# Attention exponentials of a decoder layer: the bf16 high part written by ScalarE instead of cast by VectorE

## The reference

```python
x = x + attn(layernorm(x))        # 16 query heads of width 128, one shared key and value head
x = x + experts(layernorm(x))     # 4 experts, picked by token id
x = x + ffn(layernorm(x))         # bit-quantized linear, GELU, bit-quantized linear
# inside attn, q and k normalized to length 4:
sim  = einsum('bhid,bjd->bhij', q, k)
attn = softmax(sim)
out  = einsum('bhij,bjd->bhid', attn, v)
```

## Time and profile before

| | |
|---|---|
| median of 3 runs | 1022.97 us (1019.31 to 1026.55) |
| the profiled execution | 1022.3 us |
| its span, first to last instruction | 1020.6 us |
| TensorE matmul busy | 923.6 us (90%) |
| VectorE busy | 701.5 us (69%) |
| ScalarE busy | 623.2 us (61%) |
| mean granted TensorE clock | 0.972 |

### The profile page before, as it was taken

One profiled execution on the slowest core, in us unless ns is written; L12 is line 12 of the kernel. 1 busy time (PEld: TensorE's weight loads), 2 busy tenths in 40 slices (PEclk: granted clock), 3 DMA queues, 4 the chain that ended last, 5 costly groups with the idle time before them and its releaser, 6 DMA issues.

```text
span 1020.6 us, 18975 instructions
## 1 busy us (share of the span) xinstructions
PE 923.6 (90%) x6524; PEld 519.3 (51%) x6540; DVE 701.5 (69%) x1544; ACT 623.2 (61%) x1595; POOL 272.4 (27%) x402
## 2 busy tenths in 40 slices
PE   4698899899999999999999999999847879999973
PEld 2254566556556655656656556565313334444431
DVE  6778877776886876888676767784353457777852
ACT  4666767767667756676667666664112368888550
POOL 3222212112332424324232222310240012223321
PEclk9899999999999999999999999999978989999997
DMA  8534553657768554456444434469729956444341
GB/s 237 135 73 94 115 105 82 165 146 194 178 156 197 118 141 114 109 128 121 111 97 120 104 94 120 99 140 215 173 93 175 205 120 146 98 105 106 82 103 51
DMA packets 305598, 131.85 MB, mean 129 GB/s; under 512 B 275232, under 2 KB 279840, under 8 KB 305504
## 3 DMA queue, kind: packets, MB, share of 16 engines
q1 hardware_dynamic: 301584, 117.77, 52.0%
q0 software_dynamic: 3920, 12.86, 3.8%
HBM read 42.76 MB, written 20.99 MB: 62 GB/s over the span
## 4 chain that ended last, share of the span: by engine, by line
PE 56%; DVE 18%; ACT 10%; issue 6%; DMA 5%; SPq 3%; POOL 2%; ACTq 0%; DVEq 0%; POOLq 0%
DVE P L1110 6%; PE S L673 5%; PE OUTB L685 5%; PE QB L238 4%; PE QB L239 4%; PE QB L240 4%; PE S L238 4%; PE S L239 4%; PE S L240 4%; DVE P L1108 3%; PE O L572 3%; PE O L570 3%; PE O L574 3%; PE OUTB L240 3%; PE OUTB L239 3%
## 5 line engine op out<-in xcount | busy, mean ns | idle before, releaser
L570 PE MATMUL O<-V,P 128*128 128x129 f16 x1024 | 180.5, 220 | 11.2 <-DVE OTOK L1121 9.6
L572 PE MATMUL O<-V,P 128*128 128x128 f16 x1024 | 180.6, 222 | 0.0
L574 PE MATMUL O<-V,P 128*128 128x129 f16 x1024 | 180.4, 219 | 0.0
L792 ACT ACTIVATE OTOK<-O,rd 128x128 f16<-128x128 f32 x256 | 80.6, 370 | 162.4 <-DVE rd L1115 159.0
L1108 DVE CAST P<-P 128x1024 bf16<-128x1024 f32 x128 | 88.4, 690 | 116.9 <-ACT P L781 116.9
L1110 DVE TENSOR_TENSOR P<-P 128x1024 f16<-128x1024 f32 x128 | 156.8, 1225 | 4.4
L781 ACT ACTIVATE P<-S,cst 128x1024 f32<-128x1024 f32 x128 | 139.3, 1126 | 11.9 <-PE S L240 11.3
L1427 POOL TENSOR_SCALAR qst<-qs 128x4 f32<-128x4 f32 x64 | 14.8, 232 | 434.4 <-ACT junk L764 434.4
L570 PEld LDWEIGHTS O<-V,P 128*128 128x128 bf16 x1024 | 99.0, 97 | 21.8 <-DVE P L1110 15.4
L238 PE MATMUL S<-XQA,KT 128*128 128x512 f16 x256 | 97.7, 382 | 9.0 <-DMA XQA<-P 8.1
L572 PEld LDWEIGHTS O<-V,P 128*128 128x128 bf16 x1024 | 99.7, 97 | 6.4
(11 more groups left out here) (210 smaller groups left out, 1906.2 us busy)
## 6 DMA issues: line engine op xcount, KB each, us to landing
SIDE<-in_L_ffn_w_dram SPq DMA_DIRECT2D x64, 256.0 KB, 3.0
OTA<-sorted_rows SPq DMA_DIRECT2D x4, 1028.0 KB, 7.0
OTA<-in_L_attn_Wq_dram SPq DMA_DIRECT2D x4, 1024.0 KB, 6.9
SIDE<-in_L_attn_Wout_dram SPq DMA_DIRECT2D x16, 256.0 KB, 3.1
SIDE<-in_ctx_dram SPq DMA_DIRECT2D x16, 256.0 KB
ctx_split<-SIDE SPq DMA_DIRECT2D x16, 256.0 KB
ROWB<-in_x_dram SPq DMA_DIRECT2D x16, 256.0 KB, 3.0
w_tern<-SIDE SPq DMA_DIRECT2D x32, 128.0 KB
```

What stands on the lines that cost most here:

```text
L570: nc.tensor.matmul(o, ph(g)[:, a:a + P], V[:, b % 2, j, 0:129], start=j == 0, stop=False)
L572: nc.tensor.matmul(o[:, 0:128], ph(g)[:, a:a + P], V[:, b % 2, j, 130:258], start=False, stop=False)
L574: last = nc.tensor.matmul(o, pl(g)[:, a:a + P], V[:, b % 2, j, 0:129], start=False, stop=j == NT - 1)
L792: last = nc.scalar.activation(OTOK[:, g % 2, t * P:(t + 1) * P], o_tile(t), ACT.Copy, scale=rd[:, g % 2, t:t + 1])
```

## The change

In each half of each head ScalarE runs the exponential of S twice, first into the bf16 high part and then into P32. The signal that the high part is there (`p_hi`) comes from ScalarE, and VectorE's cast of P32 is gone. The wait that guards the reuse of the two-fold high part (`o_ps`, the values of head g-2 are done) is now on ScalarE as well; on VectorE it stays ahead of the low part.

```diff
                 act.wait_ge(s_ps, 2 * g + half + 1)
                 if g >= 1:
                     act.wait_ge(p_lo, 2 * (g - 1) + half + 1)
-                nc.scalar.activation(P32[:, half * 1024:(half + 1) * 1024], S[:, half * 1024:(half + 1) * 1024],
-                                     ACT.Exp, bias=off_p).then_inc(p_exp, 1)
+                cols = slice(half * 1024, (half + 1) * 1024)
+                if g >= 2:
+                    act.wait_ge(o_ps, 2 * (g - 1))
+                nc.scalar.activation(ph(g)[:, cols], S[:, cols], ACT.Exp, bias=off_p).then_inc(p_hi, 1)
+                nc.scalar.activation(P32[:, cols], S[:, cols], ACT.Exp, bias=off_p).then_inc(p_exp, 1)
...
                 cols = slice(half * 1024, (half + 1) * 1024)
-                nc.vector.tensor_copy(ph(g)[:, cols], P32[:, cols]).then_inc(p_hi, 1)
                 dve.wait_ge(p_hi, 2 * g + half + 1)
                 nc.vector.tensor_tensor(pl(g)[:, cols], P32[:, cols], ph(g)[:, cols], ALU.subtract
                                         ).then_inc(p_lo, 1)
```

## The result

The changed kernel takes 1071.91 us (median of 4, 1068.56 to 1075.5) against 1024.76 us (median of 4, 1019.31 to 1027.7): a ratio of 1.0467, with a 95% interval of 1.0406 to 1.0528. That is 47 us slower. The profiled execution took 1075.5 us with a span of 1073.8 us. It is the slowest of its four, and the profiled one before (1022.3 us) is faster than its median, so the two profiles lie 53 us apart and not 47.

What follows compares the result with a forecast made beforehand. The ring was taken to bound sequence 0, and TensorE the heads from 16 on. Terms of 20.3 + 14.7 + 14.8 + 1.9 = 51.7 us on the profiled 1022.3 gave 1074 us, range 1062 to 1092.

Steps and rivals of the forecast that it cites:

- The ring: Attention's closed ScalarE-VectorE-ScalarE wait chain, once per head: 7.94 us plus side work, growing to 9.22 plus side work; chance 0.72.
- sequence 0: Attention's first heads, before head 16, paced by the ring: 15 turns at 1.28 us plus corrections, 20.3 us longer.
- heads 16-31: Sequence 1 of attention: heads with much side work exceed TensorE's 10.52 us, 14.7 us added.
- heads 32-57: Later attention heads: nine with 1.57 to 2.09 us excess, seven of about 0.3, 14.8 us added.
- heads 58-63 and the last low part: End of attention, without queries: the last low part and values(63) come later, 1.9 us added.
- The first head: Start of sequence 0: adds about 0.8 us, since its halves are apart already.
- The last turn: End of sequence 0: TensorE, late with queries at the lower clock, adds about 0.8 us.
- rival C: After new TensorE gaps the lower clock slows queries in 16 heads, 1.7 us each, 27 more: 1101 us, chance 0.08.
- A: From g = 16 TensorE's work covers the change; only sequence 0 and the end pay: 1044 us, chance 0.08.
- B: In sequence 0 VectorE's own queue sets the turn, so 15 turns give back 21.6 us: 1001 us, chance 0.03.
- D: Attention's second exponentials lose overlap or the extra wait breaks it: 2.26 + 0.2 us per head, 1092 us, chance 0.06.

Runs made afterwards that it cites:

- the run with filled gap: Kernel before plus three scratch exponentials per head in ScalarE's idle time ahead of head_high's second half: 1024.46 us, ratio 0.9999.
- the order alone: Changed kernel with query_high run between the exponentials of the two halves, ScalarE's work unchanged: 1028.68 us, ratio 1.005.

## Why the prediction was right

It said 1074 us, 51.7 over the profiled execution; measured are 1071.91, and 47 over before. That the total is off by only 2 us is in part luck: the growth was forecast 4.6 us too large, and it was added to an execution that lay 2.5 us under the median.

*The ring.* That the 159 us of ScalarE's idle time are a link and not room was the main step, and the run with filled gap shows it: 2.2 us per head there cost nothing, while 2.0 us per head among the exponentials cost 89 us. That the order alone takes 43 of the 47 us away again shows the same from the other side.

*The terms.* 2.00 us for two more exponentials was measured at 2.00 (starts 144.84 to 148.82, less the pair that was there); the output type makes next to no difference (1133 and 1140 ns). Less 0.72 for the cast, the ring was to grow by 1.28 and grew by 1.27. By stage:

| | forecast | profile |
|---|---|---|
| sequence 0 | 20.3 | 18.5 |
| heads 16-31 | 14.7 | 15.3 |
| heads 32-57 | 14.8 | 13.1 |
| heads 58-63 and the last low part | 1.9 | 1.8 |

The last is 0.2 us for heads 58 to 62 and 1.6 for the last low part, which ended 7.76 us after head 63's scores and now ends 9.31 us after them. In sequence 0 the forecast is 1.8 us too high, and the sum says where. Of its 15 turns eleven grew by 1.26 to 1.28 us. The first head added 0.3 us and not 0.8. Three early turns were longer than the ring before, by 1.3 us in all, and lost that; the forecast had only one of them, at 0.5. The last turn was to grow by 0.8 more than the others, since TensorE waits there for `query_low`, which comes 2.0 us later and not 1.28; but its queries at the lower clock took 4.0 us in place of 4.3, and it grew by only 0.4 more.

In heads 16 to 31 the agreement holds 1.7 us, at most, that the sum did not have: the queries of one head at the lower clock (rival C below). In heads 32 to 57 the forecast had nine heads 1.57 to 2.09 us longer; the profile has seven, 1.52 to 2.04 us. One of those too many is head 43, which follows a head with much side work but holds `keys_values`, whose 2.62 us of TensorE work cover the wait. Which the other was isn't on record.

*What it got wrong.* It said that ScalarE would still idle about 2.4 us before L795. The idle time fell from 162.4 to 114.0 us in all, 0.76 us a head, and to 1.9 us in the head shown: the cast was inside that wait and left with it. The experiments tell the two parts apart: 116.2 us with the cast left out alone, 162.8 with the second exponential alone. It also said that ScalarE would work 128 us more, and the page has 117, since rows that overlap count once there. The sum uses neither statement. And `queries(g+6)` waits for `query_low(g+5)` from g = 15 on, not 14 as the part on the kernel before has it; nothing rests on that.

*The rivals.* A (TensorE covers it from g = 16) is refuted by the stages: 28 us of the profile's growth are there. B (VectorE is the pace of sequence 0) is refuted: sequence 0 got 18.5 us longer though VectorE had less to do, and with the cast gone and nothing added, sequence 0 gained 10.8 us, half of what B needs. C (the clock) is there from g = 16, but once, not in 16 heads. It is head 23 on TensorE in the changed kernel:

```profile
308.98 0.39 PE L238 MATMUL QB<-WQA,XQA 128*128 128x512 f16 x1 [2.44 <-DVE QTOKR L1101]
...
311.54 0.63 PE L239 MATMUL QB<-WQA,XQA 128*128 128x512 f16 x1
311.96 0.63 PE L240 MATMUL QB<-WQA,XQA 128*128 128x512 f16 x1
...
313.26 0.38 PE L238 MATMUL S<-XQA,KT 128*128 128x512 f16 x1
```

After a gap of 2.44 us two matmuls are 0.42 us apart in place of 0.22 (1.2 GHz), and the twelve queries take 4.28 us in place of 2.59. That is 1.7 us, at most, of the 15.3. In heads 32 to 57 the granted clock was 1.00 throughout, with gaps up to 1.9 us. With the longer gaps of the second exponential alone, rival C came true in five heads; it was real, and sized too large for this change. In sequence 0 it fell from 0.97 to 0.95, where TensorE mostly has room. D (lost overlap, or the added wait costing time) is refuted by the starts 1.00 us apart.

## What to carry to other kernels

Follow an engine's idle time back to who ends it, and that one's wait back again. If the chain comes home to the idle engine within one turn, the idle time is a link. Work put elsewhere in the chain then costs its full length in every turn in which the chain is the longest thing (128 us of exponentials cost 89 here), while work put into the gap is free as long as it fits. Then price the chain against the busiest engine, head by head, because side work makes some turns longer than others and an average hides them. Before work is moved from one engine to another, look at the order inside the chain: the reciprocal taken earlier was worth 12 us here without any other change, and with `query_high` moved as well the change itself made no difference that could be measured.

## What the runs showed of the hardware

The lower clock does not follow from the length of the last gap alone. In the changed kernel a gap of TensorE of 2.44 us was followed by queries at 1.2 GHz, while ten others of 1.3 to 1.9 us, in heads 16 to 57, were not; with the second exponential alone a gap of 2.12 us was (4.22 us for the twelve queries), and one of 3.11 us was not (2.60 us). Exponentials of 128x1024 follow each other at 1.00 us although each has a row of 1.13, also when waits that are already met stand between them, and the same PSUM half read a second time costs no more than the first time (1133 and 1140 ns). And the stages after attention differ by some 8 us between profiles of kernels that are the same there (325.3 to 333.5 us). That is as much as the executions of one kernel differ (1019.31 to 1027.7 us before); whether it is the same spread, and what makes it, was not looked into.
